# Vector recurrence in twelve segments, rescaling inside the determinant chain, clipping pass on GpSimd, fills between steps

## What is computed

```python
h = jnp.maximum(_layernorm(x, axis=-1), 0.0)
degv = A.sum(axis=0) + A.sum(axis=1) - jnp.diagonal(A)
Ln = dinv[:, None] * (jnp.diag(degv) - A) * dinv[None, :]
_, U = jnp.linalg.eigh(Ln)
agg = jnp.einsum('vn,bvd->bnd', U, h)
x1 = jax.nn.relu(agg @ W1 + b1) @ W2 + b2
g_x = _maxpool2(_pw_conv(x1, g_w, g_b)).transpose(0, 2, 1)
theta_x = _pw_conv(x1, th_w, th_b).transpose(0, 2, 1)
phi_x = _maxpool2(_pw_conv(x1, ph_w, ph_b))
y = softmax(theta_x @ phi_x) @ g_x            # 1024 x 512 scores
z = batchnorm(_pw_conv(y.transpose, wo_w, wo_b)) + x1
out = x + einsum('nv,bvd->bnd', U, z) + z
```

## Time and profile before

| | us |
|---|---|
| median of 3 runs | 3405.35 (3404.03 to 3417.64) |
| the profiled execution | 3414.81 |
| its span | 3412.6 |
| `reflect` steps | about 20 to 482 |
| DVE alone with the eigenvalues and vectors, ACT with the rest of the layer norm | 482 to about 721 |
| first matmul of the main loop | 728.83 |
| main loop | 729 to 3412.6 |

### The profile page before, as it was taken

One profiled execution on the slowest core, in us unless ns is written; L12 is line 12 of the kernel. 1 busy time (PEld: TensorE's weight loads), 2 busy tenths in 40 slices (PEclk: granted clock), 3 DMA queues, 4 the chain that ended last, 5 costly groups with the idle time before them and its releaser, 6 DMA issues.

```text
span 3412.6 us, 66625 instructions
## 1 busy us (share of the span) xinstructions
PE 3235.3 (95%) x16512; PEld 2604.2 (76%) x16512; DVE 2318.8 (68%) x6125; ACT 2411.8 (71%) x4381; POOL 1942.8 (57%) x2069
## 2 busy tenths in 40 slices
PE   6888887779999999999999999999999999999997
PEld 4777776657777777777777777777777777777775
DVE  5777778976666666666666666666666666666664
ACT  4777889957666666667666666676666666667665
POOL 4333320126666666666666666666666666666665
PEclk9998999989999999999999999999999999999998
DMA  2233334412222222222222222222222222222222
GB/s 79 79 82 82 93 95 114 112 41 65 70 74 77 70 70 76 70 70 70 76 75 70 70 76 70 70 70 76 75 70 70 75 70 70 70 77 74 70 71 69
DMA packets 111579, 256.28 MB, mean 75 GB/s; under 512 B 47500, under 2 KB 49797, under 8 KB 111493
## 3 DMA queue, kind: packets, MB, share of 16 engines
q1 hardware_dynamic: 111493, 255.25, 27.2%
HBM read 190.69 MB, written 63.44 MB: 74 GB/s over the span
## 4 chain that ended last, share of the span: by engine, by line
PE 81%; DVE 11%; POOL 3%; issue 3%; ACT 1%; DVEq 0%; ACTq 0%; POOLq 0%
PE ps_M L781 8%; PE ps_M L782 8%; PE ps_M L783 8%; PE ps_S L858 7%; PE ps_E L781 7%; PE ps_O L781 7%; PE ps_O L783 7%; PE ps_E L782 7%; PE ps_E L783 7%; PE ps_O L782 7%; PE ps_M L842 3%; PE ps_m L680 1%; POOL sc L435 1%; PE ps_S L863 1%; PE ps_M L797 1%
## 5 line engine op out<-in xcount | busy, mean ns | idle before, releaser
L487 POOL TENSOR_TENSOR p_lo<-p,p_hi 128x512 fp32r<-128x512 f32 x1024 | 1374.3, 1342 | 936.0 <-ACT p_hi L639 931.8
L634 ACT ACTIVATE p<-ps_E 128x512 f32<-128x512 f32 x1024 | 613.5, 599 | 333.0 <-PE ps_E L783 307.6
L1324 DVE TENSOR_REDUCE nmx<-ps_S 128x1 f32<-128x512 f32 x1024 | 658.3, 684 | 130.2 <-PE ps_S L858 127.3
L639 ACT ACTIVATE p_hi<-p 128x512 fp32r<-128x512 f32 x1024 | 647.0, 632 | 32.7
L781 PE MATMUL ps_E<-o_hi,Q_hi 123*128 123x512 f32 x1024 | 426.9, 417 | 0.0
L781 PE MATMUL ps_O<-p_hi,v_hi 128*121 128x512 f32 x1024 | 406.9, 397 | 4.6 <-POOL p_lo L487 4.6
L783 PE MATMUL ps_O<-p_lo,v_hi 128*121 128x512 f32 x1024 | 406.3, 397 | 0.0
L782 PE MATMUL ps_E<-o_hi,Q_lo 123*128 123x512 f32 x1024 | 404.2, 395 | 0.0
L783 PE MATMUL ps_E<-o_lo,Q_hi 123*128 123x512 f32 x1024 | 404.0, 394 | 0.0
L782 PE MATMUL ps_O<-p_hi,v_lo 128*121 128x512 f32 x1024 | 403.8, 394 | 0.0
L1304 DVE TENSOR_REDUCE gf<-ps_M 128x256 f32<-128x512 f32 x256 | 177.0, 691 | 261.9 <-PE ps_M L783 261.9
(11 more groups left out here) (355 smaller groups left out, 6101.3 us busy)
## 6 DMA issues: line engine op xcount, KB each, us to landing
rbc<-r_dram SPq DMA_DIRECT2D x128, 484.0 KB
xin<-in_x_dram SPq DMA_DIRECT2D x128, 480.0 KB, 4.2
xt<-in_x_dram SPq DMA_DIRECT2D x128, 480.0 KB, 5.0
out_dram<-y SPq DMA_DIRECT2D x128, 480.0 KB, 3.8
o_hi<-mrow SPq DMA_DIRECT2D x256, 2.0 KB
dcol<-y SPq DMA_DIRECT2D x128, 4.0 KB, 2.0
r_dram<-rcol SPq DMA_DIRECT2D x128, 4.0 KB, 1.4
W1s<-in_L_gnn_W_dram SPq DMA_DIRECT2D x1, 512.0 KB, 4.1
```

Of the source, the lines that this page charges most:

```text
L487: pool.tensor_tensor(p_lo[:, c % 4, :], p[:, c % 4, :], p_hi[:, c % 4, :].bitcast(F32), ALU.subtract).then_inc(plo_sb, 1)
L634: act.activation(p[:, c % 4, :], ps_E[c % 2][:, :], ACT.Exp).then_inc(p_sb, 1)
L639: act.activation(p_hi[:, c % 4, :], p[:, c % 4, :], ACT.Copy).then_inc(phi_sb, 1)
L1324: dve.tensor_reduce(nmx[:, c:c + 1], ps_S[SBANK[c]][:, :], AX.X, ALU.max, negate=True).then_inc(max_sb, 1)
```

## The change

- **Vector recurrence.** The 119 steps of two elements give way to ten steps of 48 elements: each of twelve segments (and both ends) starts from the two unit vectors in PB. A rescale of 24 numbers, eleven short joins of two instructions (PX, PC), and two wide instructions (PW, PS) put the products together. The tiles lie in parts of SP and SA.
- **Determinant chain.** The shift of all 60 rows in one instruction of 2880 elements becomes 30 of 96 elements, inside the steps. The rescaling is spread over five steps each eighth step, and goes into the weights SW and one row of SA instead of into the chain's own rows.
- **Clipping.** ACT's `b_relu` becomes `relu(s)` on GpSimd, a `tensor_scalar` (add, max) over 120x1024. 76 of them stand between the `shift(k)` of the `reflect` steps, 52 behind. `xin` has three buffers. `relu(0)` stands right behind `shift(0)`.
- **Fills.** `consts` is signalled behind 15 small instructions; the wide fills stand in `fill(k)` between steps and signal `filled`.
- **Small moves.** The sum over wn stands behind `reflect`; GRID_AT is 89 instead of 91; all of `rstds` stands behind the last clip, and its second half ahead of the fill of `xt`.

The diff, cut to its core:

```diff
+            def relu(s):
+
+                pool.wait_ge(mean_done, s + 1)
+                late(pool, tr_done, s - 1)
+                pool.tensor_scalar(frelu[:, s % 2, :], xin[:, s % 3, :], lns[:, s % 4:s % 4 + 1], 0.0, ALU.add,
+                                   ALU.max).then_inc(relu_done, 1)
...
+            cleared = 0
             for k in range(STEPS):
                 shift(k)
+                fill(k)
+                while cleared < (placed(k) - 4) // 6 + 2:
+                    relu(cleared)
+                    cleared += 1
...
-            for level in range(7):
-                masked(level)
...
+            for s in range(cleared, B):
+                relu(s)
+                if s >= WY_SLOT + 3 and (s - WY_SLOT - 3) % 2 == 0 and (s - WY_SLOT - 3) // 2 < 7:
+                    masked((s - WY_SLOT - 3) // 2)
             rstds(0, B // 2)
...
+            rstds(B // 2, B)
             pool.wait_ge(wy_ps, WY_P(7) + 1)
             pool.memset(xt[0:1, :, :], 0.0).then_inc(xt_free, 1)
-            rstds(B // 2, B)
...
+            def slot(k):
+                if k < B:
+                    b_sq(k)
+                if k + 1 < B:
+                    b_sum(k + 1)
+                if 0 <= k - 2 < B:
+                    b_ft(k - 2, k % 2)
+                if 0 <= k - 4 < B:
+                    b_p1(k - 4, k % 2)
...
+                    if s % 2 and s + 2 < HALF:
+                        rows = shifted(s + 2)
+                    if phase == 0:
+                        sized = did(dve.tensor_reduce(size, SP[:, s - 1:s + 1, :, :].rearrange("p s e k -> p e s k"), AX.XY,
+                                                      ALU.max, apply_absolute_value=True))
...
+            for i in range(2, SEG + 2):
+                need(made)
+                turned = did(T(turn_, seg(AV, i), PB[:, i - 1, :, :, :], ALU.mult))
+                if i + 1 < SEG + 2:
+                    mark(T(thin(i + 1), seg(E2P, i + 1), PB[:, i - 1, :, :, :], ALU.mult))
+                need(turned)
+                made = did(T(PB[:, i, :, :, :], turn_, thin(i), ALU.subtract))
...
+            for g in range(NSEG - 1):
+                step(T(PX, MG[:, :, g, :, :].rearrange("p r e b -> p e r b"),
+                       PC[:, g, :, :].unsqueeze(2).to_broadcast([N, 2, 2, 2]), ALU.mult))
+                step(T(PC[:, g + 1, :, :], PX[:, :, :, 0], PX[:, :, :, 1], ALU.add))
...
-GRID_AT = 91
+GRID_AT = 89
```

More of the change, by code:

```diff
@@ L219, in build @@
         xcol_ready = sem("xcol_ready")
-        x_in = [sem(f"x_in{i}") for i in range(2)]
+        x_in = [sem(f"x_in{i}") for i in range(3)]
         mean_done = sem("mean_done")
@@ L323, in _, with load @@
                          b1.rearrange("(a c j) -> a c j", a=1, c=1).to_broadcast([1, B + 1, H])).then_inc(b1_in, 16)
[L325 to L334, removed]
+            def load(k):
+                late(sp, sq_done, k - 2)
+                late(sp, relu_done, k - 2)
+                sp.dma_start(xin[:, k % 3, :], x[k:k + 1, :, :].rearrange("a n d -> n (a d)")).then_inc(x_in[k % 3], 16)
+            for k in range(B):
+                load(k)
+            sp.wait_ge(filled, 1)
             sp.wait_ge(b2_split, 2)
@@ L388, in chain @@
                 pool.wait_ge(pool_step, n[0])
-            for t, v in ((ident, 0.0), (strict, 1.0), (sub, 0.0), (ones, 1.0), (u, 0.0), (zw, 0.0),
-                         (srow, 0.0), (EB, 0.0), (CM, 0.0), (Uaug, 1.0), (rstd, 1.0)):
+            for t, v in ((ident, 0.0), (strict, 1.0), (sub, 0.0), (ones, 1.0), (u, 0.0), (zw, 0.0), (rstd, 1.0)):
                 chain(pool.memset(t[:, :], v))
[L393 to L402, removed]
             for i, v in enumerate((-0.5, BN_EPS)):
@@ L423, in _ @@
-            pool.wait_ge(b2_split, 1)
-            pool.tensor_tensor(b2lo[:, :], b2f[:, :], b2hi[:, :].bitcast(F32), ALU.subtract).then_inc(b2_split, 1)
+            pool.affine_select(out=sub[:, :], in_=sub[:, :], compare_op=ALU.not_equal, fill=1.0,
+                               base=-1, pattern=[[-1, N]], channel_multiplier=1).then_inc(consts, 1)
             pool.wait_ge(dve_out, 1)
             pool.tensor_tensor(colA[:, 6:7], colA[:, 5:6], colA[:, 10:11], ALU.pow).then_inc(pool_out, 1)
+            for t, v in ((srow, 0.0), (EB, 0.0), (CM, 0.0), (Uaug, 1.0), (Cop, 0.0), (IA, 0.0), (X, 0.0)):
+                chain(pool.memset(t[:, :], v))
@@ L581, in factor @@
                     keep((QA[:, N:2 * N], ps_V[0:N, 128:128 + N], 1.0))
[L583 to L588, removed]
+            for k in range(B + 4):
+                slot(k)
+                if WY_SLOT <= k < WY_SLOT + WY_STEPS:
                     factor(k - WY_SLOT)
@@ L1066, in minors, with need @@
+            def need(i):
+                dve.wait_ge(dve_step, i)
             def minors():
                 e2 = lambda s: E2P[:, s, :].unsqueeze(2).to_broadcast([N, 2, K])
[L1070 to L1073, removed]
@@ new lines, in _ @@
+            need(made)
+            step(dve.tensor_reduce(PM, PB[:, SEG:SEG + 2, :, :, :].rearrange("p r g e b -> p (g e) r b"), AX.XY, ALU.max,
+                                   apply_absolute_value=True))
+            step(TS(PM, PM, TINY, None, ALU.max))
+            step(dve.reciprocal(PM, PM))
+            step(T(MG.rearrange("p r g e b -> p r (g e) b"), PB[:, SEG:SEG + 2, :, :, :].rearrange("p r g e b -> p r (g e) b"),
+                   PM.unsqueeze(1).unsqueeze(3).to_broadcast([N, 2, 2 * NSEG, 2]), ALU.mult))
```

213 lines of the change are left out of this document (123 added, 90 removed).

## The result

| | before | changed |
|---|---|---|
| median of the runs, us | 3411.49 (4 runs, 3404.03 to 3420.24) | 3546.44 (4 runs, 3544.86 to 3548.21) |
| span of the profiled execution | 3412.6 | 3543.0 |
| end of the `reflect` steps | 482.2 | 607.1 |
| first matmul of the main loop | 728.83 | 856.58 |
| from there to the end | 2683.8 | 2686.4 |

The ratio is 1.0395, 95% interval 1.0363 to 1.0426: 135 us slower. The prediction had 3431, with 3368 to 3490. The sign was right; the size was wrong by a factor of five.

A forecast was written before the change was run, and what follows sets the result against it. It took a chain across engines to bound `reflect`, with ACT and DVE busy behind it. Terms -3 + 50 - 9.3 - 4.5 - 44.3 + 35 + 2 = +26 us on 3405.35 gave 3431 us, range 3368 to 3490.

The forecast's parts named there:

- The step that failed: Price of one clip on GpSimd, taken as 1.1 us though no row had such an instruction.
- The bounds: Limits for the clip's price: a fill of 1024 elements, 0.95 us, and two subtractions of 512 with two inputs, 2.7.
- The rival of the slow clip: A clip on GpSimd takes 1.5 us or more; 1.5 gives 3482 us; chance 13%.
- Its other rule: Each 0.1 us of a clip beyond 1.1 costs 12.8 us over 128 clips while they hold DVE.
- DVE's hold: DVE's two-input instructions stand while a GpSimd clip reads: 0.66 us for each of 76 in `reflect`, 50 us.
- Vectors: The vector recurrence on DVE behind `reflect` falls from 57.05 to 12.7 us, -44.3 us.
- Determinant passes: DVE's passes behind `reflect`, with short shifts and spread rescaling: about 1.5 to 1.7 us saved, three times, -4.5 us.
- Grid: DVE's 9.27 us wait for PE behind `reflect` goes and PE waits for DVE instead, -9.3 us.
- Fills: At the start: 10 us earlier was possible, but `relu(0)` stands between `shift(0)` and `shift(1)`; -3 us.
- The end: GpSimd's queue ahead of the main loop: xt is free later, b2 lands last, +2 us.
- the rival without exclusion: GpSimd's and DVE's reads take turns at no visible cost; GpSimd's order at the end bounds; 3358 us, chance 15%.
- two clip terms: DVE held by GpSimd's clips: +50 us for 76 in `reflect`, +35 us for 52 behind it.

The follow-up runs named there:

- act_clip: The changed kernel with the clip given back to ACT in its old place, no clip on GpSimd; 3397.0 us, ratio 0.9963.
- forms: act_clip with eight kinds of idle GpSimd instruction by turns at the places of the changed kernel's clips; 3502.2 us in a single run.
- dead_fill: act_clip with 74 idle fills of a 120x1024 tile on GpSimd at the changed kernel's clip places; 3401.9 us, ratio 0.9978.
- dead_copy: act_clip with 74 idle copies of a 120x1024 tile on GpSimd at the changed kernel's clip places; 3482.3 us, ratio 1.0201.
- dead_clip: act_clip with 74 idle clips on GpSimd at the changed kernel's clip places, nobody waiting for them; 3530.7 us, ratio 1.0357.

## Why the prediction was wrong, point by point

**The step that failed** is one sentence: "It has one input and writes as much as the fill, so I take 1.1." A clip takes 3.75. The form `tensor_scalar` on 1024 elements was in no row, and I closed the gap by what the instruction moves, not by what it computes. The bounds, a fill and two subtractions of two tiles, didn't hold it either. A row of the same form was at hand, the two-operation `tensor_scalar` of 64 elements with 0.24 us, but the form takes 0.22 on a single element too, and nothing about a long one could be read from it.

**The rival of the slow clip** had the mechanism: beyond 1.69 us "`shift` is late too". With 3.75 its rule gives 76 x 2.06 = 157 for `reflect`. The traces show 75 steps that grew from 3.91 to 5.75 in the mean, 138 us (8 of them in the one step that waits for the first x), and 42 that shrank by 0.1 each. It is less than 157 because a mean step of before has 3.91 us and not the 3.4 of the late one that I read; it left GpSimd 2.1 us. I gave this rival 13%, and placed it at 1.5 us. Its other rule, 12.8 us for each 0.1 beyond 1.1 while clips hold DVE, would give 339: it took the hold to last as long as the clip, and it lasts about 1.0 us (below).

**DVE's hold**, the forecast's main term, exists. In the idle copy, of the length that I had assumed, it is 0.85 us where it meets DVE and 0.61 in the mean, 45 us in all: the 0.66 and 50 of the forecast were nearly right. But the steps grow by 0.97 and `reflect` by 83 us, since DVE also waits 44 us more for PE, for which the sum had no term. So even with a clip of 1.1 us the forecast would have been too low. In the changed kernel DVE is held as long (339.2 to 388.0 us busy), and it costs next to nothing in `reflect`, because DVE is early there: the sign of the forecast came out right for another reason than its own. Behind `reflect`, 60 of DVE's instructions between 606 and 826 us are longer than the shortest of their kind by over 0.15 us, together by 42.7: 0.82 for each of 52 clips, where the prediction had 0.67 and 35. (To its last minimum DVE takes 216.0 us there and 174.0 in `act_clip` with the same instructions, 42.0 more.)

**Vectors.** Predicted 12.7 from 57.05. In `act_clip` from 628.21 to 640.62, 12.4; in the changed kernel 15.6 with clips beside it. Right.

**Determinant passes.** Predicted -4.5. From PE's answer to the last value LAM, with two of the passes in between, DVE takes 96.9 us before (549.21 to 646.12) and 97.5 in `act_clip` (530.36 to 627.84). So nothing was gained. The 29 short shifts of a pass are dearer than I had scaled them down from the wide one, 0.25 us instead of 0.17, 7.4 instead of 4.9 (this group of `act_clip` has three passes):

```profile
L1099 DVE TENSOR_TENSOR SA<-DP,X 120x96 f32<-120x96 f32 x87 | 22.1, 254 | 0.3
```

The 0.07 us "to get going" in that price came from no row; an instruction of 4 elements has 0.16 in the earlier trace rows. With the measured 7.4 the prediction's own sum for a pass turns from a gain of 1.7 into a loss of 0.8 (3.0 - 7.4 + 3.6), and the measured loss is 0.3.

**Grid.** Predicted: the 9.27 us of the earlier trace rows go and PE waits 15 to 20 instead. In the changed kernel PE waits 18.8 us for DVE there. Right.

**Fills.** Predicted -3, because `relu(0)` blocks `shift(1)`. It does, at 23.66 instead of 20.2, again because the clip is 3.7; against before 0.6 us are left of the 10.

**The end.** Predicted: b2's landing is last, +2. It is last. But clips on a slow GpSimd end at 827.8, and then the power for the length waits for the first `rstds`: from DVE's last minimum at 823.1 to the main loop there are 33.5 us, before 20.2, so +13. I had described just this order in the rival without exclusion, and had not asked whether a long clip brings it about as well.

**Sum.** `reflect` +124.9, DVE's part -10.4 (-8.6 grid, where 0.65 of the 9.27 are left, -44.6 vectors, +42.7 holds, the rest small), the end +13.3, the main loop +2.6: +130.4. The forecast had +47, -23, +2 and 0 in the same places.

**What nobody waits for.** Without its two clip terms the forecast's sum is 3346. `act_clip` shows 3397, but it is no test of that sum: the prediction had taken 1.05 us a slot off ACT, and in `act_clip` ACT keeps them. There ACT has no gap behind `reflect` (220.00 of 220 us, above; 226.6 of 227 before), and nobody waits for DVE. The change's 52 us on DVE could pay only if ACT was relieved, and the relief went to an engine that is three times slower at it (3.75 us against ACT's 1.17).

## To carry to other kernels

Where a change moves an operation to another engine and no row shows that operation there at that size, its price is open by a factor and not by some per cent: give the case beyond your upper bound a chance that fits, and ask first from which length on the engine is late. Before costing what a mover saves, list the engines that are full in the stretch; a gain on one of two engines that end together is worth nothing until the other is relieved. And a long instruction on an engine that others call for short answers costs them its length less their slack each time, whoever reads the result. One that fits into the slack can cost as well: each idle copy of 1.04 us made the kernel 1.15 us longer, each idle fill of 0.95 us hardly anything.

## What the runs showed of the hardware

- On GpSimd, 120x1024 fp32: fill 0.95 us, copy 1.04, add with two inputs 1.90, `tensor_scalar` with one operation 2.79 (constant) or 2.90 (pointer), with two 3.66 or 3.74; 512 elements with two 2.03, 64 elements 0.24, one element 0.22.
- The hold isn't as long as the GpSimd instruction. Beside the idle copy, and beside the add with two inputs in `forms`, DVE stood up to its end. Beside the two-operation `tensor_scalar` of 3.72 us it stood only until about 1.0 us behind its start (560.15 to 561.2 above), and then ran freely with two inputs for the other 2.7. In the changed kernel 427 of the 435 two-input instructions of DVE that start in the last 1.1 us of a clip keep their time.
- A second hold, at the end of a GpSimd `tensor_scalar`, meets another kind of DVE instruction, a `tensor_scalar` of its own. In the changed kernel nine of the 15 that start in the last 1.1 us of a clip stand to its end, and the eight two-input instructions that are late there each stand right behind one of them. Two clips back to back, the first of which ends at 687.35:

```profile
683.65 7.38 POOL L448 TENSOR_SCALAR frelu<-xin,lns 120x1024 f32<-120x1024 f32 x2
...
686.39 0.99 DVE L1130 TENSOR_SCALAR SR<-SR 120x2 f32<-120x2 f32 x1
686.47 0.92 DVE L1142 TENSOR_TENSOR SP<-ST,SM 120x48 f32<-120x48 f32 x1
...
687.44 1.07 DVE L1118 TENSOR_TENSOR ST<-SA,SP 120x48 f32<-120x48 f32 x1
```

  The last row is the first hold of the second clip. Beside the one-operation form in `forms` it is the same, with 0.96 instead of 0.2 us:

```profile
472.79 2.87 POOL L475 TENSOR_SCALAR xt<-W2f,ones 120x1024 f32<-120x1024 f32 x1
...
473.13 0.77 DVE L1039 TENSOR_TENSOR u<-sc,u 1x1 f32<-1x1 f32 x1
...
474.73 0.96 DVE L1056 TENSOR_SCALAR cs<-u,sc 1x24 f32<-1x24 f32 x1
```

  The Trainium skill, in the section of "SBUF — State Buffer" that is named above, calls the shared ports an exclusive lock and says, of DVE's two-port modes, that whoever issues first has them for the whole instruction. For the copy the trace agrees, for the long `tensor_scalar` it doesn't, and the measurement decides here.
- TensorE's granted clock fell wherever the steps grew. Between 100 us and the end of `reflect` it was 0.96 in `act_clip` and 0.95 in `dead_fill` (6.8 and 6.7 matmuls a us), 0.76 in `dead_copy` (5.6) and 0.71 in `dead_clip` (5.1): the lower of the two levels, 1.2 instead of 2.4 GHz, for about half of the time. In `dead_copy` four matmuls of the layer norm then took 1.21 us (from 407.44) and stood ahead of the chain's own, for which DVE waited 1.25; its steps without a copy took 4.12 instead of 3.95. The 45 us of hold and the 44 us of longer waits for PE are read from one trace; that the lower clock follows from the hold, and that it is all of PE's part, isn't shown: no kernel here held the one and left the other.
